# Gating the second batch's opening behind the first batch's scores, with an early Ln and an identity burst on TensorE, in an MoE–attention–MoE kernel

## The chip, the cores and the metric

The kernel runs on one core of a Trainium2 chip. The metric is the device time of one execution in microseconds (us); lower is better. The figures for the kernel before are three runs, and one more execution that was profiled. Engines are TensorE (PE; its weight loads are PEld), VectorE (DVE), ScalarE (ACT), GpSimd (POOL) and SyncE (SP, here only a DMA queue).

## What is computed

x is 8 batches of 512 rows with 128 features, all in float32. Three residual steps follow each other:

```python
x = x + 0.5 * ffn(layernorm(x), gate_w, fc_w, proj_w)   # 8 experts, each row uses its best 2
x = x + attention(layernorm(x), Wq, Wkv, Wout, bout, rel_emb)
x = x + 0.5 * ffn(layernorm(x), gate_w, fc_w, proj_w)

q = (x @ Wq) ...            # 16 heads of 64
k, v = split(x @ Wkv)       # one k and one v of 64 columns, shared by all heads
sim = q k^T * scale + bias  # bias by relative position, causal mask
out = softmax(sim) v ; out @ Wout + bout
```

The change touches the passage from the first step to the second: the opening of the attention.

## The kernel before, in words

**The expert stages** (`ffn_sp`, `ffn_pool`, `ffn_act`, `ffn_dve`, `ffn_pe`, called with 0 and with 1) sort all rows by expert into 72 tiles of 128 rows, and run up-projection (L1363), Gelu (L834), down-projection (L1373) and a copy (L1120, signalled by `yo_done`) tile by tile. In the first of them each result tile goes to `y1_dram`.

**The attention** is cut into small tasks, named by kind, batch b and place. The kinds that matter here, with engine and line:

- `GA(b,q)` on POOL (L762): two indirect gathers per 128 rows of a batch, which fetch the rows' two expert results into `yg`; the buffer holds one batch, so `GA(b+1)` waits for `CB(b)`.
- `CB(b,z)` on DVE (L1213, L1218): adds the weighted results to `x_sb`, four instructions for each half of a batch.
- `LS(b)` (DVE, L913 to L935) takes the row statistics and signals `ln_var`; `LA(b)` (ACT, `ln_act`, L803 and L805) takes Ln and Exp of the variance; `LN(b)` (DVE, L942 to L946 and L1231) makes the normalised rows `xa`.
- `BO(b)` on POOL (L769): adds the output bias to `x_sb`.
- `xT(b)` (PE, L1404) transposes `xa`; `xTh` (ACT, L859) and `xTl` (DVE, L1235) split the result in a high and a low part.
- `K`, `V`, `Q(b,g,c)` (PE, L1296 to L1298, three matmuls for each product) and their copies `KH`, `VC`, `QH` (ACT, L862, L865, L869) and `KL`, `QL` (DVE, L1238, L1243).
- For each of 16 units n (four head groups g, in each four row tiles t): `S` (PE, L1431) makes scores of four heads, `TTR` (DVE, L1253) adds the bias and takes the maximum, `EXP` (ACT, L874), `R` (DVE, L1260) the reciprocal of the sums, `N` (POOL, L789) the normalisation, `T` (PE, L1440) the transposes, `TC` their copy (ACT L881 or DVE L1266), `AV` (PE, L1456), `O` (ACT, L887), `Y` (PE, L1463), `YA` (DVE, L1275).

**The order of the work** is written out by a planner when the kernel is built. `attention_tasks` lists each task with a cost and with what it needs. `attention_order` walks through time with these costs: whenever an engine is free it gives it, of the tasks whose needs are met, the one with the smallest due time from `wanted_at`. The due time of `CB(1)`, `LS(1)` and `LN(1)` lies far behind that of the scores of batch 0, but a task with met needs is started at once when its engine is free. The result, `ORDER`, is one fixed list for each engine. On the chip each engine follows its list strictly, and waits on semaphores for the data of the other engines; the needs listed in the planner shape the lists, and the semaphore waits in the code are those of the data. Scores take two of four PSUM banks called "front", which K, V, Q and xT also use.

PE's list begins right behind `ffn_pe(0)`; ACT's behind the last Gelu; POOL's behind a wait for the last write of `y1_dram`.

Of the kernel before, what the change touches and what calls it, by code (L numbers as in the profile page):

```python
# [9 lines left out]
P = 128  # L10
D = 128
BATCH, SEQ = 8, 512
TILES = BATCH * SEQ // P
# [3 lines left out]
ETILES = TILES * TOPK + E  # L17
PAIRS = TILES * TOPK
H, DH = 16, 64
HG, NG = 4, 4  # L20
QT = SEQ // P
# [25 lines left out]
ACT = mybir.ActivationFunctionType  # L47
# [24 lines left out]
def build(nc, x, Wq, Wkv, Wout, bout, rel_emb, gate_w, fc_w, proj_w, out):  # L72
    ctx = ExitStack()
    with ctx:
        def sb(name, shape, dt=F32):
            return ctx.enter_context(nc.sbuf_tensor(name, shape, dt))

        def sem(name):
            return ctx.enter_context(nc.semaphore(name))
# [11 lines left out]
        ident = sb("ident", [P, P])  # L91
# [16 lines left out]
        lnt = sb("lnt", [P, 6, TILES])  # L108
# [4 lines left out]
        eps_t = sb("eps_t", [P, 1])  # L113
# [62 lines left out]
        with att:  # L176
# [33 lines left out]
        bank = [ctx.enter_context(nc.psum_tensor(f"bank{i}", [P, 512], F32)) for i in range(8)]  # L210
# [10 lines left out]
        ln_var = sem("ln_var")  # L221
# [12 lines left out]
        xrT_ps, xrT_done, up_ps, gelu_done, y_ps, yo_done = (  # L234
            sem(n) for n in ("xrT_ps", "xrT_done", "up_ps", "gelu_done", "y_ps", "yo_done"))
# [62 lines left out]
        def attention_tasks():  # L298

            tasks = {}  # L300

            def task(name, cost, needs, takes=None, frees=None, banks=1):
                tasks[name] = (cost, needs, takes and (takes, banks), frees if frees is None or type(frees[0]) is tuple else (frees, 0))

            for b in range(BATCH):
                for q in range(QT):
                    task(("GA", b, q), {"pool": 2.6}, [("CB", b - 1, q // 2)])
                for z in range(2):
                    task(("CB", b, z), {"dve": 1.6}, [("GA", b, 2 * z), ("GA", b, 2 * z + 1)])
                task(("LS", b), {"dve": 2.6}, [("CB", b, 0), ("CB", b, 1), ("LN", b - 1)])  # L310
                task(("LA", b), {"act": 3.4}, [("LS", b)])
                task(("LN", b), {"dve": 2.0}, [("xT", b - 1), ("LA", b)])
                task(("BO", b), {"pool": 1.3}, [("LN", b)])
                task(("xT", b), {"pe": 0.45}, [("LN", b), ("Q", b - 2, NG - 1, 1), ("V", b - 2), ("K", b - 2)], "front")
                task(("xTh", b), {"act": 0.48}, [("xT", b), ("Q", b - 2, NG - 1, 1), ("V", b - 2), ("K", b - 2)])
                task(("xTl", b), {"dve": 0.6}, [("xTh", b)], None, ("xT", b))
                task(("K", b), {"pe": 0.7}, [("xTl", b)] + [("S", b - 2, NU - 1, c) for c in range(2)], "front")
                task(("KH", b), {"act": 0.48}, [("K", b)] + [("S", b - 2, NU - 1, c) for c in range(2)])
                task(("KL", b), {"dve": 0.6}, [("KH", b)], None, ("K", b))
                task(("V", b), {"pe": 1.1}, [("xTl", b), ("AV", b - 2, NU - 1)], "front")  # L320
                task(("VC", b), {"act": 0.3}, [("V", b), ("AV", b - 2, NU - 1)], None, ("V", b))
                for g in range(NG):
                    for c in range(2):
                        b2, g2 = (b, g - 2) if g >= 2 else (b - 1, g - 2 + NG)
                        task(("Q", b, g, c), {"pe": 0.7}, [("xTl", b), ("S", b2, g2 * QT + QT - 1, c)], "front")
                        task(("QH", b, g, c), {"act": 0.5}, [("Q", b, g, c), ("S", b2, g2 * QT + QT - 1, c)])
                        task(("QL", b, g, c), {"dve": 0.6}, [("QH", b, g, c)], None, ("Q", b, g, c))
                for n in range(NU):
                    g, t = divmod(n, QT)
                    for c in range(2):  # L330
                        task(("S", b, n, c), {"pe": (0.34, 0.34, 0.5, 0.66)[t]},
                             [("KL", b), ("QL", b, g, c), ("T", *earlier(b, n, 8), t)], "front", None, 2)
                    for h in range(HG):
                        task(("TTR", b, n, h), {"dve": (0.28, 0.41, 0.55, 0.68)[t]}, [("S", b, n, h // 2), ("EXP", *earlier(b, n, 2), h)],
                             None, (("S", b, n, h // 2), h % 2))
                        task(("EXP", b, n, h), {"act": (0.385, 0.49, 0.6, 0.71)[t]}, [("TTR", b, n, h), ("R", *earlier(b, n, 8))])
                    task(("R", b, n), {"dve": 0.12}, [("EXP", b, n, h) for h in range(HG)] + [("N", *earlier(b, n, 8))])
                    task(("N", b, n), {"pool": (1.25, 2.1, 2.95, 3.8)[t]}, [("R", b, n)])
                    for jj in range(t + 1):
                        task(("T", b, n, jj), {"pe": 0.44}, [("N", b, n)], "turned")  # L340
                        task(("TC", b, n, jj), {"act": 0.48, "dve": 0.6}, [("T", b, n, jj), ("AV", *ring_user(b, n, jj))],
                             None, ("T", b, n, jj))
                    task(("AV", b, n), {"pe": 0.43 * (t + 1) + 0.05}, [("TC", b, n, jj) for jj in range(t + 1)] +
                         ([("VC", b)] if n == 0 else []) + [("YA", *earlier(b, n, 2))])
                    task(("O", b, n), {"act": 0.36}, [("AV", b, n), ("Y", *earlier(b, n, 2))])
                    task(("Y", b, n), {"pe": 0.45}, [("O", b, n)])
                    task(("YA", b, n), {"dve": 0.25}, [("Y", b, n), ("BO", b)])
                for q in range(QT):
                    task(("ST", b * QT + q), {"dve": 0.25}, [("YA", b, NU - QT + q)])
            for i, group in enumerate(GROUPS):  # L350
                task(("V2", i), {"dve": 1.7}, [("ST", t) for t in group])
                task(("A2", i), {"act": 3.4}, [("V2", i)])
                task(("I2", i), {"dve": 1.0}, [("A2", i)] + [("SC", t - 2 * QT) for t in group])
                for t in group:
                    task(("X2", t), {"dve": 0.34}, [("I2", i)])
                    task(("SC", t), {"pool": 2.6}, [("B2", i, 1)])
                mine = [m for m, piece in enumerate(PIECES) if piece[0] in group]
                for m in mine:
                    task(("T2", m), {"pe": 0.5}, [("X2", t) for t in PIECES[m]] + [("L2", m - 1)], "front")
                    task(("C2", m), {"act": 0.48}, [("T2", m), ("L2", m - 1)], None, ("T2", m))  # L360
                    task(("L2", m), {"pe": 0.6}, [("C2", m)], "front")
                    task(("G2", m), {"dve": 0.2}, [("L2", m), ("H2", i - 1, 1)], None, ("L2", m))
                task(("H2", i, 0), {"dve": 1.2}, [("G2", m) for m in mine] + [("B2", i - 1, 1), ("W3", i - 1)])
                task(("H2", i, 1), {"dve": 1.6}, [("H2", i, 0)])
                task(("W2", i), {"act": 0.25}, [("H2", i, 1)])
                task(("W3", i), {"dve": 0.6}, [("W2", i)])
                task(("P2", i), {"pe": 0.3}, [("H2", i, 1)], "front")
                task(("B2", i, 0), {"dve": 1.5}, [("P2", i)], None, ("P2", i))
                task(("B2", i, 1), {"dve": 1.2}, [("B2", i, 0)])
            return {k: (cost, [x for x in needs if x in tasks], takes, frees) for k, (cost, needs, takes, frees) in tasks.items()}  # L370
# [426 lines left out]
        def _(act):  # L797
            a = nc.scalar
# [35 lines left out]
                        a.activation(hT[:, n % 2, :], bank[2 + n % 2][:], ACT.Gelu).then_inc(gelu_done, 1)  # L834

            def attention_act():
                for k in ORDER["act"]:
                    kind, b = k[0], k[1]
                    if kind == "LA":
# [26 lines left out]
                    elif kind == "QH":  # L866
                        _, _, g, c = k
                        act.wait_ge(misc_ps, MISC_PS["Q", b, g, c])
                        a.activation(qst[:, g % 2, 0, c, :], BANK_OF["Q", b, g, c][:], ACT.Copy, scale=DH ** -0.5).then_inc(misc_hi, 1)  # L869
                    elif kind == "EXP":  # L870
                        _, _, n, h = k
# [4 lines left out]
                    elif kind == "TC":  # L876
                        _, _, n, jj = k
# [4 lines left out]
                    elif kind == "O":  # L882
                        _, _, n = k
# [405 lines left out]
        def _(pe):  # L1289
            t_ = nc.tensor  # L1290
# [85 lines left out]
                        ins.then_inc(y_ps, 1)  # L1376

            def attention_pe():
                for k in ORDER["pe"]:
                    kind, b = k[0], k[1]  # L1380
                    if k in BANK_OF:
# [33 lines left out]
                    elif kind == "Q":  # L1415
                        _, _, g, c = k
# [3 lines left out]
                    elif kind == "S":  # L1420
                        _, _, n, c = k
# [6 lines left out]
                        for i, (zq, zk) in enumerate(((0, 0), (0, 1), (1, 0))):  # L1428
                            for o in range(2):
                                rows = slice(o * DH, (o + 1) * DH)  # L1430
                                ins = t_.matmul(out[o][:, 0:w], qst[rows, g % 2, zq, c, t * P:(t + 1) * P], kst[rows, b % 2, zk, 0:w],  # L1431
                                                start=(i == 0), stop=(i == 2))
                                if i == 2:
                                    ins.then_inc(s_ps, 1)
                    elif kind == "T":
                        _, _, n, jj = k
# [5 lines left out]
                    elif kind == "AV":  # L1442
                        _, _, n = k
# [9 lines left out]
                        for jj in range(n % QT + 1):  # L1453
                            for o in range(2):
                                heads = pT[:, (b * NB + blk(n, jj)) % RING, :].rearrange("p (c o q) -> p o c q", c=2, o=2)[:, o, :, :]
                                ins = t_.matmul(BACK_BANK[n % 2][o * DH:(o + 1) * DH, 0:2 * P], vst[:, b % 2, jj, :], heads,  # L1456
                                                start=(jj == 0), stop=(jj == n % QT))
                        ins.then_inc(av_ps, 1)
                    elif kind == "Y":
                        _, _, n = k  # L1460
                        pe.wait_ge(ot_done, OT_DONE["O", b, n])
                        for c in range(2):
                            ins = t_.matmul(BACK_BANK[n % 2][:, 2 * P:2 * P + D], ot[:, n % 2, c * P:(c + 1) * P], wo_sb[:, n // QT, c, :],  # L1463
                                            start=(c == 0), stop=(c == 1))
# [26 lines left out]
```

## Time and profile before

| | |
|---|---|
| median of three runs | 1161.58 us (1161.24 to 1164.48) |
| the profiled execution | 1159.88 us |
| its span in the trace | 1157.9 us |
| PE, DVE, ACT, POOL busy, share of the span | 82%, 65%, 52%, 54% |
| mean granted TensorE clock | 0.938 of full speed |
| first expert stage | ends at 243.5 us of the span |
| attention | about 245 to 975 us |
| second expert stage and combination | to 1157.9 us |

The span is what the profiler saw of the profiled execution, 2.0 us less than that execution's time. "idle before" in a row names what ended an engine's wait. Shares over the whole span mix stages with different limits; the opening of the attention takes some 35 us of the 1157.9.

### The profile page before, as it was taken

The page shows a single profiled execution, that of the slowest core. Times are in us where ns is not written, and L with a number is a line of the kernel's source. Part 1 is how long each engine was busy: PE and PEld are TensorE (multiplying, and loading weights), DVE is VectorE, ACT ScalarE, POOL GpSimd, SP SyncE. Part 2 cuts the span into 40 slices and gives each one's busy share as a digit, 9 for nine tenths or more (in the row PEclk, how much of TensorE's full clock was granted, in tenths as well). Part 3 has the DMA queues.
Part 4 walks back from the last instruction along what each step waited for, and adds up shares of the span by engine and source line. Part 5 has one row for each costly group of instructions (what it writes and reads, how often), then busy time and mean ns, then how long its engine had stood idle before and what let it go on. Part 6 is the DMA issues. An engine that isn't in the chain of part 4 may idle for free.

```text
span 1157.9 us, 25233 instructions
## 1 busy us (share of the span) xinstructions
PE 949.3 (82%) x7670; PEld 771.9 (67%) x7670; DVE 755.4 (65%) x2652; ACT 603.8 (52%) x1627; POOL 623.1 (54%) x578
## 2 busy tenths in 40 slices
PE   1514999935989999899999899999898881999970
PEld 1514999934666767667777667776676661999970
DVE  4682222226898788978788897778878865333327
ACT  1201333314867777767788768777577661333320
POOL 2153445437677873448745559654486552455543
PEclk9996999976999999999999999999999995999995
DMA  7898888831457775200000000000000001777646
GB/s 206 127 99 256 209 211 208 200 82 44 72 90 124 126 123 105 39 5 32 4 2 2 1 13 27 2 2 1 2 29 11 1 20 51 209 204 210 202 135 198
DMA packets 105951, 106.57 MB, mean 92 GB/s; under 512 B 10034, under 2 KB 77748, under 8 KB 105824
## 3 DMA queue, kind: packets, MB, share of 16 engines
q1 hardware_dynamic: 96720, 86.41, 31.6%
q0 software_dynamic: 9104, 18.57, 7.2%
q8 instruction: 67, 1.10, 0.4%
q14 instruction: 60, 0.49, 0.2%
HBM read 65.22 MB, written 40.24 MB: 91 GB/s over the span
## 4 chain that ended last, share of the span: by engine, by line
PE 58%; DVE 19%; issue 7%; DMA 7%; SPq 3%; POOL 2%; ACT 2%; another core or an unknown queue 1%; DVEq 1%; POOLq 0%; ACTq 0%
PE bank L1431 11%; PE bank L1363 9%; PE bank L1440 9%; PE bank L1373 9%; PE bank L1456 8%; PE bank L1463 4%; DMA yg<-y_dram,pos_row 2%; DVE prob L1253 2%; DVE pT L1266 1%; PE bank L1296 1%; DMA xr<-slot_dram 1%; PE bank L1298 1%; PE bank L1297 1%; DVE x_sb L1131 1%; POOL yg L762 1%
## 5 line engine op out<-in xcount | busy, mean ns | idle before, releaser
L789 POOL TENSOR_TENSOR prob<-prob,rsum 128x256 f32<-128x256 f32 (+3 forms) x256 | 315.1, 1257 | 214.0 <-DVE rsum L1260 213.4
L874 ACT ACTIVATE prob<-prob,negmax 128x384 f32<-128x384 f32 (+3 forms) x512 | 282.4, 553 | 102.8 <-DVE negmax L1253 101.8
L1253 DVE CUSTOM_DVE_ANT_0 prob<-bank,bias_tab 128x384 f32<-128x384 f32 (+3 forms) x512 | 232.5, 484 | 55.5 <-PE bank L1431 52.6
L834 ACT ACTIVATE hT<-bank 128x512 f32<-128x512 f32 x144 | 86.0, 597 | 255.4 <-PE bank L1363 255.4
L1431 PE MATMUL bank<-kst,qst 64*128 64x256 f32 (+2 forms) x1536 | 182.4, 356 | 29.0 <-DVE negmax L1253 13.3
L1440 PE MATMUL bank<-ident,prob 128*128 128x128 f32 x1280 | 185.6, 279 | 3.4 <-ACT pT L881 3.2
L1431 PEld LDWEIGHTS bank<-kst,qst 64*128 64x128 f32 x1536 | 118.8, 191 | 86.4 <-issue 50.5
L1440 PEld LDWEIGHTS bank<-ident,prob 128*128 128x128 f32 x1280 | 145.2, 142 | 35.5 <-issue 17.3
L1120 DVE COPY yo<-bank 128x128 f32<-128x128 f32 x144 | 42.0, 291 | 194.0 <-PE bank L1373 181.5
L1456 PE MATMUL bank<-pT,vst 128*64 128x256 f32 x1280 | 165.5, 393 | 1.0 <-DVE pT L1266 0.9
L1363 PE MATMUL bank<-xrT,w1t 128*128 128x128 f32 x1152 | 155.0, 278 | 2.9 <-DMA w1t<-L_ffn_fc_w 2.3
L1373 PE MATMUL bank<-w_sb,hT 128*128 x1152 | 152.1, 275 | 0.0
L1363 PEld LDWEIGHTS bank<-xrT,w1t 128*128 128x128 f32 x1152 | 142.7, 195 | 3.4 <-issue 2.6
L1373 PEld LDWEIGHTS bank<-w_sb,hT 128*128 128x128 f32 x1152 | 140.2, 192 | 0.1
L1266 DVE COPY pT<-bank 128x512 f32<-128x512 f32 x167 | 113.5, 684 | 10.6 <-PE bank L1440 9.0
L1456 PEld LDWEIGHTS bank<-pT,vst 128*64 128x64 f32 x1280 | 82.8, 138 | 52.9 <-issue 18.0
L723 POOL DMA_INDIRECT xr<-xn_dram,gidx x72 | 68.3, 948 | 86.5 <-PE bank L1355 67.7
L730 POOL DMA_INDIRECT y_dram<-yo,sidx x72 | 70.8, 983 | 77.8 <-DVE sidx L1112 71.5
L881 ACT ACTIVATE pT<-bank 128x512 f32<-128x512 f32 x153 | 88.9, 589 | 29.5 <-PE bank L1440 28.8
L874 ACT ACTIVATION_READ_ACCUMULATOR prob<-prob,negmax 128x1 f32 x512 | 96.8, 189 | 0.0
L1463 PE MATMUL bank<-wo_sb,ot 128*128 128x128 f32 x512 | 85.3, 295 | 1.4 <-ACT ot L887 1.4
L779 POOL DMA_INDIRECT slot_dram<-slot,idx x64 | 63.4, 991 | 39.0 <-DVE idx L1207 22.6
(213 smaller groups left out, 1157.3 us busy)
## 6 DMA issues: line engine op xcount, KB each, us to landing
w1t<-L_ffn_fc_w SPq DMA_DIRECT2D x144, 256.0 KB
slot_dram<-fill SPq DMA_DIRECT2D x15, 975.0 KB
bias_dram<-hg SPq DMA_DIRECT2D x1, 5120.0 KB, 54.7
xr<-slot_dram SPq DMA_DIRECT2D x72, 65.0 KB
y_dram<-yo SPq DMA_DIRECT2D x72, 64.0 KB
bias_tab<-bias_dram SPq DMA_DIRECT2D x1, 4096.0 KB, 13.1
in_tile<-y_dram SPq DMA_DIRECT2D x8, 512.0 KB, 4.7
slot_dram<-fill SPq DMA_DIRECT2D x2, 1040.0 KB
```

The source lines that it names most:

```text
L789: g.tensor_tensor(out=pv, in0=pv, in1=rsum[:, n % 8, hs].unsqueeze(2).to_broadcast([P, 2, (n % QT + 1) * P]), op=ALU.mult).then_inc(norm_d ...
L834: a.activation(hT[:, n % 2, :], bank[2 + n % 2][:], ACT.Gelu).then_inc(gelu_done, 1)
L874: a.activation(prob[n % 8][:, h, :], prob[n % 8][:, h, :], ACT.Exp, scale=-1.0, bias=negmax[:, i % 8:i % 8 + 1], accum_out=lsum[:, n % 8, ...
L881: a.activation(pT[:, (b * NB + blk(n, jj)) % RING, :], BANK_OF["T", b, n, jj][:], ACT.Copy).then_inc(pt_act, 1)
L1253: v.tensor_tensor_reduce(out=prob[n % 8][:, h, :], in0=BANK_OF["S", b, n, h // 2][h % 2][:, 0:w], in1=bias_tab[:, HG * (n // QT) + h, SEQ ...
L1266: v.tensor_copy(pT[:, (b * NB + blk(n, jj)) % RING, :], BANK_OF["T", b, n, jj][:]).then_inc(pt_dve, 1)
L1363: ins = t_.matmul(bank[2 + n % 2][:, c * P:(c + 1) * P], w1t[:, n % 4, c * P:(c + 1) * P], xrT[:, n % 2, :], start=True, stop=True)
L1373: ins = t_.matmul(bank[6 + n % 2][:, 0:D], hT[:, n % 2, c * P:(c + 1) * P], w2_sb[:, ds(e, 1), c, :].rearrange("p a d -> p (a d)"), start= ...
L1431: ins = t_.matmul(out[o][:, 0:w], qst[rows, g % 2, zq, c, t * P:(t + 1) * P], kst[rows, b % 2, zk, 0:w], start=(i == 0), stop=(i == 2))
L1440: ins = t_.transpose(out[:, h * P:(h + 1) * P], prob[n % 8][:, h, jj * P:(jj + 1) * P], ident[:])
L1456: ins = t_.matmul(BACK_BANK[n % 2][o * DH:(o + 1) * DH, 0:2 * P], vst[:, b % 2, jj, :], heads, start=(jj == 0), stop=(jj == n % QT))
L1463: ins = t_.matmul(BACK_BANK[n % 2][:, 2 * P:2 * P + D], ot[:, n % 2, c * P:(c + 1) * P], wo_sb[:, n // QT, c, :], start=(c == 0), stop=(c ...
```

## The change

Four edits. In the planner, `CB(1,z)` also needs `QL(0,0,1)` and `KL(0)`; `BO(0)` also needs `KL(0)`; `xT(1)` also needs `N(0,4)`, the normalisation of the first unit of the second head group. ACT's list is preceded by one Ln of the 128x1 tile `eps_t` into a cell of `lnt`. PE's list is preceded by 12 matmuls of the identity with itself into bank 7, behind a wait for the last `yo` copy and for `LS(0)` (`ln_var` 2). The `GA` tasks of batch 2 need `CB(1)` as before, and so come later too.

```diff
@@ attention_tasks
                 for z in range(2):
-                    task(("CB", b, z), {"dve": 1.6}, [("GA", b, 2 * z), ("GA", b, 2 * z + 1)])
+                    opened = [("QL", 0, 0, 1), ("KL", 0)] if b == 1 else []
+                    task(("CB", b, z), {"dve": 1.6}, [("GA", b, 2 * z), ("GA", b, 2 * z + 1)] + opened)
...
-                task(("BO", b), {"pool": 1.3}, [("LN", b)])
-                task(("xT", b), {"pe": 0.45}, [("LN", b), ("Q", b - 2, NG - 1, 1), ("V", b - 2), ("K", b - 2)], "front")
+                task(("BO", b), {"pool": 1.3}, [("LN", b)] + ([("KL", 0)] if b == 0 else []))
+                task(("xT", b), {"pe": 0.45}, [("LN", b), ("Q", b - 2, NG - 1, 1), ("V", b - 2), ("K", b - 2)] +
+                     ([("N", 0, QT)] if b == 1 else []), "front")
@@ attention_act
+                a.activation(lnt[:, 3, TILES - 1:TILES], eps_t[:], ACT.Ln, bias=eps_t[:, 0:1])
                 for k in ORDER["act"]:
@@ attention_pe
+                pe.wait_ge(yo_done, ETILES)
+                pe.wait_ge(ln_var, 2)
+                for _ in range(12):
+                    t_.matmul(bank[7][:, 0:P], ident[:], ident[:], start=True, stop=True)
                 for k in ORDER["pe"]:
```

## Rows read from the trace of the kernel before

**Rows 1.** Page, part 1: busy time, share and instructions of the engines.
```profile
PE 949.3 (82%) x7670; PEld 771.9 (67%) x7670; DVE 755.4 (65%) x2652; ACT 603.8 (52%) x1627; POOL 623.1 (54%) x578
```
**Rows 2.** Busy time by stretch: length, PE, PEld, DVE, ACT, POOL, clock, DMA.
```profile
243.50:265.00 21.50, 0.11 (x1) 0.14 (x2) 7.39 (x32) 1.78 (x3) 14.63 (x16) 0.59 0.18 48
278.80:345.00 66.20, 58.03 (x407) 41.13 (x408) 58.70 (x200) 45.86 (x140) 45.12 (x40) 0.87 0.42 75
345.00:880.00 535.00, 511.03 (x4097) 375.11 (x4096) 443.27 (x1535) 398.00 (x1171) 333.47 (x287) 0.98 0.19 35
```
**Rows 3.** Chain that ended last, 230 to 300 us: start, length, what.
```profile
264.55 2.60 DMA yg<-y_dram,pos_row
...
267.53 2.31 DVE x_sb L1218 x2
...
275.32 1.28 ACT L803
```
**Rows 4.** Timeline of ACT, 241 to 283 us: start, length, instruction, idle before.
```profile
241.89 1.28 ACT L803 ACT_TABLE_LOAD   x1
259.99 0.30 ACT L803 ACTIVATE lnt<-lnt,eps_t 128x4 f32<-128x4 f32 x1 [16.82 <-DVE lnt L935]
...
261.60 0.20 ACT L805 ACTIVATE lnt<-lnt 128x4 f32<-128x4 f32 x1
...
274.70 0.60 ACT L862 ACTIVATE kst<-bank 128x512 fp32r<-128x512 f32 x1 [0.65 <-PE bank L1298]
...
278.34 0.37 ACT L865 ACTIVATE vst<-bank 128x256 f32<-128x256 f32 x1
```
**Rows 5.** Timeline of DVE, 241 to 283 us.
```profile
262.31 0.61 DVE L1218 SCALAR_TENSOR_TENSOR x_sb<-yg,gw,x_sb 128x128 f32<-128x128 f32 x2
262.83 0.15 DVE L942 TENSOR_TENSOR lnt<-lnt 128x4 f32<-128x4 f32 x1
...
282.01 0.69 DVE L1235 TENSOR_TENSOR xTl<-bank,xTh 128x512 fp32r<-128x512 f32 x1
```
**Rows 6.** Timeline of PE, 241 to 283 us.
```profile
264.89 1.09 PE L1404 MATMUL bank<-ident,xa 128*128 128x128 f32 x4 [21.73 <-DVE xa L1231]
270.49 0.80 PE L1296 MATMUL bank<-xTh,wqs 128*128 128x512 f32 x1 [4.52 <-DVE xTl L1235]
...
275.76 0.47 PE L1296 MATMUL bank<-xTh,wqs 128*128 128x512 f32 x1
...
277.00 0.40 PE L1298 MATMUL bank<-xTh,wqs 128*128 128x512 f32 x1
278.80 0.63 PE L1431 MATMUL bank<-kst,qst 64*128 64x256 f32 x6 [1.41 <-issue]
280.64 0.66 PE L1404 MATMUL bank<-ident,xa 128*128 128x128 f32 x4 [1.21 <-DVE negmax L1253]
```
**Rows 7.** Page, part 5: the up-projection's matmuls.
```profile
L1363 PE MATMUL bank<-xrT,w1t 128*128 128x128 f32 x1152 | 155.0, 278 | 2.9 <-DMA w1t<-L_ffn_fc_w 2.3
```
**Rows 8.** Timeline of PE where the second expert stage begins.
```profile
981.68 1.92 PE L1363 MATMUL bank<-xrT,w1t 128*128 128x128 f32 x8
983.46 0.48 PE L1355 MATMUL bank<-ident,xr 128*128 128x128 f32 x1
...
985.98 1.06 PE L1363 MATMUL bank<-xrT,w1t 128*128 128x128 f32 x8
```
**Rows 9.** PE by stretch of 1 us: length, busy, granted clock, DMA.
```profile
274.00:275.00 1.00, 1.00 (x8) 0.75 0.12 33
984.00:985.00 1.00, 1.00 (x9) 0.76 0.81 200
```
**Rows 10.** Timelines of POOL and DVE: the bias addition, and two steps of LS(2).
```profile
268.09 1.27 POOL L769 TENSOR_TENSOR x_sb<-x_sb,bout_sb 128x512 f32<-128x512 f32 x1
...
299.92 1.20 DVE L926 TENSOR_TENSOR lnt<-stats 128x4 f32<-128x4 f32 x1
...
301.12 1.86 DVE L928 TENSOR_TENSOR lnt<-stats 128x4 f32<-128x4 f32 x1
```

## The prediction

> **What bounds the kernel now.** I read the engines' shares first. PE leads with 82% and no other engine passes 65% [rows 1], but that mean hides the stage at issue, so I went on to the busy time by stretch [rows 2]. From 345 to 880 us PE is busy 511 of 535 us: there PE bounds, and a head start that reaches that stretch should be kept. From the last expert copy to 265 us PE does nothing, while the first batch is fetched and normalised. From the first score (278.80) to 345 both PE (58.0 of 66.2 us) and DVE (58.7) are nearly full, and the granted clock averages only 0.87, so nearly 9 us of that stretch's full-clock work is missing.
>
> The chain of waits tells what holds the first scores back [rows 3]: a gather of batch 1 (264.55, 2.60 us), DVE's combination of batch 1 (267.53, 2.31 us), and later a table load for batch 1's Ln on ACT (275.32). None of the three belongs to batch 0. The timelines of ACT, DVE and PE [rows 4 to 6] show the same: each engine follows a fixed list, and batch 1 stands in it ahead of batch 0.
>
> **The change part by part.**
>
> *CB(1) behind KL(0).* The first Exp ends at 261.80 [rows 4], but DVE begins LN(0) at 262.83 behind CB(1,0) [rows 5]. Without it LN(0) starts at about 261.82, and the transposes, at 264.89 before [rows 6], could start at 263.88: 1.0 us. After xTh DVE then stood in CB(1,1) until 269.84. Without that, from transposes to the first Q takes what batch 1 needs from its own transposes to the end of xTl: 280.64 to 282.70, 2.06 us [rows 5, 6], and 0.04 us to start. Before it was 270.49 − 264.89 = 5.60 us. That is 3.5 us more.
>
> *Late LA(1).* It goes with CB(1). Before, ACT ended KH at 275.30, then ran Ln, Exp and two table loads of batch 1, and copied V only at 278.34 [rows 3, 4]. The scores start right behind that copy, at 278.80, because it frees a bank. K's low part needs 0.60 us on ACT for KH and 0.69 us on DVE for KL (xTl's price, same size) [rows 4, 5], with hops 1.34 us after K ends. So S could follow K by 1.4 us; before it was 278.80 − 274.68 = 4.1.
>
> *The early Ln.* The table load of the first Ln stands at 241.89, and the Ln itself waits until 259.99 with the table in place [rows 4]. The load was ahead of the wait already. The added Ln takes the load over and runs some 0.3 us in 16.8 us of idle time: 0 us either way, and as much as nothing if that cover went. The later Ln and Exp loads remain. The Trainium skill ("ScalarE: Activation LUTs", What ACT_TABLE_LOAD costs) puts a switch of tables at about 2.66 us; and it says under What happens when an exp ACTIVATE runs that the compiler places the load right before the activation. Read so, the early Ln would take 2.66 us out of batch 0's path and the sum below would be 1153.3 instead of 1156.0; the row at 241.89 speaks against it and is what I follow.
>
> *The identity burst.* A float32 matmul shows as two records: 1152 records [rows 7] for 72 tiles, 2 stages and 4 matmuls each. So 12 matmuls are 24 records. Eight cost 983.46 − 981.68 = 1.78 us at the low clock, and about 0.9 us at the high one (1.06 us with the last one's tail) [rows 8]. The burst starts with LS(0)'s end, at 260.0. All at the low level (1.2 GHz) it lasts 5.3 us. But the clock rose to the high level (2.4 GHz) about 2.8 us after such matmuls began at 981.68, and 4.0 us after the Q products began at 270.49 [rows 6, 8, 9]. With 4.0 us, 18 records run low and 6 high: 4.7 us, to 264.7. The transposes wanted 263.88, so the burst costs 0.8 us (0.3 to 1.4). In return Q, Q, K run high: three matmuls at 512 columns cost (277.00 − 275.76)/5 = 0.25 us each, so nine take 2.25 us [rows 6], where they took 4.2 us (270.49 to 274.68): 1.9 us won.
>
> *The first score*: 264.7 + 2.06 + 0.04 + 2.25 + 1.4 = 270.4 or 270.5. Before 278.80: **8.3 us earlier** (6.4 us if the clock has fallen again by then).
>
> *What is then behind it.* The moved work does not vanish. CB(1), eight instructions of 0.31 us by its undisturbed row (two in 0.61) [rows 5], is 2.5 us. LS(1) is about 1.9 us (258.05 to 259.96, by LA(0)'s start) [rows 4]. Both lay before 278.8 and come behind the first score: 4.4 us of DVE. They now also meet POOL. Beside BO(0) two L1218 took 2.3 us instead of 0.6 [rows 3, 5, 10], and BO(0) is released by the same KL(0) as CB(1): up to 1.8 us again. Two steps of LS(2) took 1.20 and 1.86 us [rows 10] where such a step takes 0.15 (L942) [rows 5]: 2.7 us, which I put on LS(1) and as bound on LN(1). Up to 7.2 us, down to 0 if POOL is idle just then; I take half, 3.6. Sum on DVE: 8.0 us. The Trainium skill ("GPSIMD Engine Reference", Specifications) says that the two engines share their way to SBUF and contend when a DVE instruction has two SBUF inputs; these three kinds have, the scores' L1253 reads PSUM. The rows at 267.53 and 301.12 agree.
>
> Against that DVE was idle 66.2 − 58.7 = 7.5 us of this stretch [rows 2]; I let half of it, 3.7, be filled. DVE alone would keep 8.3 + 3.7 − 8.0 = 4.0 us. PE alone would keep all 8.3: its work is only shifted (xT(1), K(1), V(1) were all behind 278.8), and from 281 on it ran at the low clock, part of which may be recovered. POOL's eight gathers of GA(2), about 1.25 us apart, move behind the scores as well; POOL is idle 21 of 66 us, and N has the earlier due time, so 0 us. SP's fills wait for output tiles and only shift. xT(1) behind N(0,4) asks for nothing near its use: batch 1's scores come some 80 us later.
>
> **Sum.** Between 4.0 and 8.3 I take 5.6, nearer DVE, since it is the fuller engine up to 345 us. Profiled execution 1159.9 − 5.6 = 1154.3; the median lies 1.7 higher, so 1156.0. About 0.3%, 3.5 us, is what a measurement here can tell from no change.
>
> **The rivals.**
>
> 1. *Forecast* (0.46): 8 us earlier scores, some 4 to 8 kept; 1153.5 to 1158.0.
> 2. *All kept and the clock too* (0.13). If the high level also holds behind the first score, part of the missing 9 us comes back: 8.3 + 3 = 11, 1150. For: no low-clock K(1) and V(1) in the first scores. Against: the first scores leave PE half idle until transposes come, and with such gaps the clock fell at 281.
> 3. *Given back on DVE, or a burst without effect* (0.24). If the clock doesn't rise in the burst or falls before Q, the burst ends at 265.3 and Q, Q, K take 4.2: 2.5 us of the gain go, 1158.5. If the stretched steps are at their bound, about the same. The planner also re-orders everything later, which may add or take some 3 us.
> 4. *Slower* (0.17): DVE as the wall. LS(1) and LN(1) sit in DVE's list amid TTR and wait on POOL's port for the full 7.2 us, none of the idle time is filled, and the clock is low at the scores: 6.4 − 4.4 − 7.2 = −5.2, so 1166.8. It decides from the point at which moved and stretched work outgrow the 6.4 to 8.3 us. For: DVE is already the fullest engine there. Against: its idle time lies right behind the first scores.
>
> That the early Ln does nothing is part of all of them.
>
> **How the numbers follow.** Faster takes case 1 nearly whole and case 2: 0.58. Same is case 3, with the edge of case 1: 0.25. Slower is case 4: 0.17. The likeliest case gives 1156.0. The range reaches from case 2 (1149.5) to just short of case 4's price (1165.0).
>
> **What would show it.** Ln's table load at about 241.9 as before. 24 identity records from 260.0, the clock rising at 263 to 264. Transposes at 264.7, first Q near 266.8 and no L1213 ahead of it. First score at 270 to 271. CB(1) beside BO(0), with L1218 stretched. DVE nearly full from 271 to 340, and every later landmark (first AV, last AV of the attention) some 5 us earlier. The prediction is wrong if the first score is early but the last AV isn't, or if the burst is still running when xa is ready by more than 1.5 us.

## The result, and the profile after

| | before | after |
|---|---|---|
| median of three runs | 1161.58 us | 1150.08 us (1149.36 to 1152.96) |
| profiled execution | 1159.88 us | 1152.96 us |
| its span | 1157.9 us | 1151.1 us |
| mean granted clock | 0.938 | 0.948 |

The ratio is 0.9893, with a 95% interval of 0.9871 to 0.9916: the change makes the kernel 11.5 us faster, where 5.6 were forecast. The profiled execution of after was the slowest of its three, so the two traces differ by only 6.8 us of span.

The opening, engine by engine, from the profile of each execution. ACT and POOL of the changed kernel first (start, length, instruction, idle before it); line numbers have moved by two to seven against those of before.

```profile
242.94 1.28 ACT L839 ACT_TABLE_LOAD   x1
244.24 0.29 ACT L839 ACTIVATE lnt<-eps_t 128x1 f32<-128x1 f32 x1
260.93 0.30 ACT L805 ACTIVATE lnt<-lnt,eps_t 128x4 f32<-128x4 f32 x1 [16.39 <-DVE lnt L938]
...
266.98 0.60 ACT L862 ACTIVATE xTh<-bank 128x512 fp32r<-128x512 f32 x1 [4.24 <-PE bank L1411]
...
271.99 0.39 ACT L868 ACTIVATE vst<-bank 128x256 f32<-128x256 f32 x1 [0.66 <-PE bank L1301]
```
```profile
266.58 1.27 POOL L771 TENSOR_TENSOR x_sb<-x_sb,bout_sb 128x512 f32<-128x512 f32 x1
273.37 0.96 POOL L764 DMA_INDIRECT yg<-y_dram,pos_row  x1 [5.51 <-DVE x_sb L1221]
```

The table load stands where it stood before [rows 4], just behind the last Gelu; only its owner is new. V's copy (271.99) no longer waits behind batch 1's Ln and Exp. The bias addition BO(0) runs at 266.58, some five microseconds *ahead* of the KL(0) that it "needs" (271.36, below): a need in the planner shapes lists, and in POOL's list BO(0) stands right behind the gathers of batch 1.

DVE and PE of the changed kernel, the same columns:

```profile
262.84 0.16 DVE L945 TENSOR_TENSOR lnt<-lnt 128x4 f32<-128x4 f32 x1 [1.95 <-ACT lnt L807]
...
267.61 0.69 DVE L1238 TENSOR_TENSOR xTl<-bank,xTh 128x512 fp32r<-128x512 f32 x1 [2.85 <-ACT xTh L862]
...
271.36 0.69 DVE L1241 TENSOR_TENSOR kst<-bank,kst 128x512 fp32r<-128x512 f32 x1
271.97 0.60 DVE L1216 SCALAR_TENSOR_TENSOR x_sb<-yg,gw,x_sb 128x128 f32<-128x128 f32 x2
272.49 0.61 DVE L1221 SCALAR_TENSOR_TENSOR x_sb<-yg,gw,x_sb 128x128 f32<-128x128 f32 x2
...
284.75 1.86 DVE L929 TENSOR_TENSOR lnt<-stats 128x4 f32<-128x4 f32 x1
```
```profile
261.04 5.46 PE L1385 MATMUL bank<-ident 128*128 128x128 f32 x24 [16.82 <-DVE lnt L938]
266.29 0.65 PE L1411 MATMUL bank<-ident,xa 128*128 128x128 f32 x4
268.35 0.50 PE L1299 MATMUL bank<-xTh,wqs 128*128 128x512 f32 x1 [1.41 <-DVE xTl L1238]
...
272.66 0.62 PE L1438 MATMUL bank<-kst,qst 64*128 64x256 f32 x6
```

On DVE, ACT and PE no instruction of batch 1 is left between LS(0) and KL(0); POOL's gathers of batch 1 still run there. The first half of CB(1) follows KL(0) at once and stands ahead of the first score, the second half comes at 275.86, both at their undisturbed price. The burst ran wholly at the low clock; Q ran high (three records in 0.70 us). The first score stands at 272.66. This execution's first expert stage, untouched by the change, ended 1.06 us later (last `yo` copy at 244.26, before at 243.20), so I count from there: the first score came at 35.6 us before, and comes at 28.4 us.

To see where the time goes from there I take landmarks: the starts of the first, fourth, 16th, 32nd, 64th, 104th and last of the 128 output additions YA (L1275 of before), in us from the start of the last `yo` copy. They are read from the traces by their place in DVE's list, one traced execution for each kernel.

| | first score | tile 1 | tile 4 | tile 16 | tile 32 | tile 64 | tile 104 | tile 128 |
|---|---|---|---|---|---|---|---|---|
| before | 35.6 | 60.9 | 81.6 | 139.1 | 220.6 | 385.5 | 596.2 | 710.7 |
| after | 28.4 | 43.7 | 64.9 | 123.3 | 205.9 | 372.5 | 583.3 | 701.7 |
| lead | 7.2 | 17.2 | 16.7 | 15.8 | 14.7 | 13.0 | 12.9 | 9.0 |

The lead at the first score more than doubles until the fourth tile, and is then slowly paid back.

How much of such a lead is chance can be read from kernels of the experiments below whose four lists are those of before as far as tile 16 (e7, e11, and e4 but for its one early Ln). Their fourth tile came at 85.3 (e7), 82.9 (e11) and 85.3 us (e4), where the table has 81.6; their tile 32 at 222.7, 223.1 and 223.2, where it has 220.6. The clock differed: after the end of the expert stage it first rose at about 294 us of the span in e4 and e7, and at 274.5 in before. Four traces of the changed opening (after, e1, e8, e12) lie within 1.0 us at tile 4. So the trace of before is the quickest of its kind, and a lead over it is a low reading by up to 3.7 us at tile 4 and 2.6 at tile 32.

The same passages by the busy time of the engines (length, PE, PEld, DVE, ACT, POOL, clock, DMA share, GB/s): to the first score, to tile 4, to tile 16, to tile 32. Before:

```profile
243.20:278.80 35.60, 7.99 (x31) 6.17 (x32) 16.02 (x57) 7.61 (x13) 25.19 (x27) 0.62 0.18 48
278.80:324.80 46.00, 39.64 (x263) 28.25 (x265) 38.94 (x136) 31.74 (x95) 29.09 (x26) 0.85 0.30 56
324.80:382.30 57.50, 54.49 (x424) 39.12 (x425) 50.93 (x168) 41.75 (x122) 43.67 (x41) 0.94 0.73 122
382.30:463.80 81.50, 78.00 (x625) 57.06 (x623) 68.87 (x234) 60.86 (x186) 54.67 (x48) 0.98 0.66 114
```

After:

```profile
244.26:272.70 28.44, 10.25 (x54) 9.26 (x54) 9.70 (x35) 4.84 (x9) 16.40 (x17) 0.70 0.16 42
272.70:309.10 36.40, 31.14 (x249) 21.56 (x248) 34.68 (x127) 29.46 (x91) 29.34 (x26) 1.00 0.38 71
309.10:367.60 58.50, 56.43 (x449) 41.06 (x447) 55.93 (x187) 45.49 (x129) 44.14 (x42) 1.00 0.70 119
367.60:450.20 82.60, 78.73 (x625) 56.17 (x624) 70.42 (x243) 62.67 (x188) 63.02 (x56) 0.98 0.71 121
```

The second passage is where the forecast went wrong. It shrank from 46.0 to 36.4 us; PE is busy 8.5 us less in it and DVE 4.3 us less, and the clock is at its high level (2.4 GHz) throughout. DVE is now the fuller engine there, busy for 34.68 of 36.40 us. The third and fourth passages are each about 1 us longer.

What left the second passage is seen by the same kind of landmark. Before, K(1) and V(1) ran in it (V's copy at 44.7), and so did LS(2) and, at 78.2, the xa of LN(2). After, V(1) is copied at 111.0, CB(2) begins at 60.4 instead of 32.7 (it moved *into* the passage), and LN(2) comes at 96.1, behind tile 4. The gates name only batches 0 and 1; they pushed *everything* that runs ahead back by a step. They also re-ordered batch 0 itself: before, PE's list had the first transpose behind S(0,3,0) and the first AV behind Q(0,2,0); after, the first transpose stands behind S(0,2,1) and the first AV ahead of Q(0,2,0).

### The profile page after: what moved, and what is told of

It reads as the page before. It is cut to its first block, busy times and chain, and to the rows that moved or that the text cites. A ratio compares the mean times of both kernels' runs of the same rounds, so it can differ in the third digit from the quotient of the medians.

```text
span 1151.1 us, 25281 instructions
## 1 busy us (share of the span) xinstructions
PE 951.7 (83%) x7694; PEld 773.8 (67%) x7694; DVE 752.4 (65%) x2650; ACT 605.7 (53%) x1630; POOL 623.2 (54%) x578
## 4 chain that ended last, share of the span: by engine, by line
PE 61%; DVE 19%; issue 7%; DMA 4%; SPq 3%; ACT 2%; POOL 1%; another core or an unknown queue 1%; DVEq 0%; POOLq 0%; ACTq 0%
PE bank L1438 11%; PE bank L1447 10%; PE bank L1366 10%; PE bank L1463 9%; PE bank L1376 9%; PE bank L1470 4%; DVE prob L1256 2%; DVE x_sb L1216 2%; PE bank L1299 2%; DMA xr<-slot_dram 1%; PE bank L1301 1%; PE bank L1300 1%; DVE x_sb L1134 1%; DVE pT L1269 1%; PE bank L1358 1%
## 5 line engine op out<-in xcount | busy, mean ns | idle before, releaser
L1438 PE MATMUL bank<-kst,qst 64*128 64x256 f32 (+2 forms) x1536 | 179.1, 351 | 29.8 <-DVE negmax L1256 15.0
L1447 PE MATMUL bank<-ident,prob 128*128 128x128 f32 x1280 | 188.4, 282 | 2.1 <-ACT pT L884 1.9
L1447 PEld LDWEIGHTS bank<-ident,prob 128*128 128x128 f32 x1280 | 146.3, 143 | 34.1 <-issue 18.4
L1269 DVE COPY pT<-bank 128x512 f32<-128x512 f32 x165 | 111.6, 683 | 12.3 <-PE bank L1447 10.8
L732 POOL DMA_INDIRECT y_dram<-yo,sidx x72 | 70.8, 984 | 79.2 <-DVE sidx L1115 72.8
```

What stands on the lines that cost most here:

```text
L1269: v.tensor_copy(pT[:, (b * NB + blk(n, jj)) % RING, :], BANK_OF["T", b, n, jj][:]).then_inc(pt_dve, 1)
L1447: ins = t_.transpose(out[:, h * P:(h + 1) * P], prob[n % 8][:, h, jj * P:(jj + 1) * P], ident[:])
```

## The experiments

Ratios are against runs of the kernel before on the same chip; a ratio is not the quotient of the two medians (for e1 0.9849 against 0.9868), so differences in us that are given from medians are a second, rougher reading. A tile or score is timed from the last `yo` copy, as above.

**The parts of the change.**

`e1_again` is the changed kernel unaltered.

> The changed kernel once more, on the chip of the three others. Measured so far: 11.5 us under the kernel before (0.9893). Every theory expects 9 to 14 us under it again.

Measured: 1149.28 against 1164.66 us, ratio 0.9849 (0.979 to 0.9909). That is a little more than the 9 to 14 us expected. Its lead was 17.3 us at tile 4, 15.5 at tile 32 and 12.3 at tile 128.

`e2_gates_only`:

```diff
-                a.activation(lnt[:, 3, TILES - 1:TILES], eps_t[:], ACT.Ln, bias=eps_t[:, 0:1])
...
-                pe.wait_ge(yo_done, ETILES)
-                pe.wait_ge(ln_var, 2)
-                for _ in range(12):
-                    t_.matmul(bank[7][:, 0:P], ident[:], ident[:], start=True, stop=True)
```

> The three gates in the planner alone, no early Ln and no burst. Theory A (the gates carry the gain, because batch 1's K and V products and its Ln no longer stand among the first scores; the clock follows by itself): 8 to 12 us under the kernel before, first score near 271 us plus the shift of the stage, clock high from about 276. Theory B (the burst carries a good part by holding the clock high through the first scores): 2 to 6 us under it, with low-clock slices between 270 and 290.

Measured: 1150.13 us against 1164.66, ratio 0.9864 (0.9804 to 0.9924), more than the 8 to 12 us of theory A. The gates carry the gain. PE by stretches of 5 us (length, busy, clock, DMA share, GB/s):

```profile
270.00:275.00 5.00, 5.00 (x24) 0.70 0.00 0
275.00:280.00 5.00, 2.95 (x27) 0.98 0.17 41
280.00:285.00 5.00, 4.91 (x30) 0.68 0.16 39
285.00:290.00 5.00, 4.31 (x30) 1.00 0.02 3
```

Without the burst Q and K run low and the clock falls once more at about 280. The first score comes at 29.7 instead of 28.4 us, tile 4 at 66.4 instead of 64.9 (after) or 64.3 (e1); but at tile 32 it is 205.7 against 205.9 and 205.1. The burst's microsecond is used up by then. The medians differ by 0.85 us, which these intervals can't tell from nothing.

`e3_burst_only` puts the burst alone on the lists of before:

```diff
             def attention_pe():
+                pe.wait_ge(yo_done, ETILES)
+                pe.wait_ge(ln_var, 2)
+                for _ in range(12):
+                    t_.matmul(bank[7][:, 0:P], ident[:], ident[:], start=True, stop=True)
```

> The burst alone on the lists of the kernel before. Theory A: within 1.5 us of the kernel before, since CB(1) and LA(1) still stand in the way and the clock falls again at the gap of 4 us before the first Q. Theory B: 3 to 6 us under it, clock high through 281 to 295 where it was low.

Measured: 1163.8 us against 1164.66, ratio 0.9998 (0.9967 to 1.0029). The clock rose, and fell again before the first Q:

```profile
265.00:270.00 5.00, 1.33 (x10) 0.84 0.20 52
270.00:275.00 5.00, 4.07 (x10) 0.50 0.16 39
```

`e4_ln_only` adds the early Ln alone:

```diff
             def attention_act():
+                a.activation(lnt[:, 3, TILES - 1:TILES], eps_t[:], ACT.Ln, bias=eps_t[:, 0:1])
```

> The early Ln alone. The prediction's reading of the row at 241.89 says 0 us (within 1). The reading by which the load stood in batch 0's path says 1.3 to 2.7 us under the kernel before.

Measured: ratio 1.0003 (0.9969 to 1.0036), median 1167.48 us with a wide spread (1157.47 to 1173.09). The early Ln is worth nothing that shows.

Two of the three gates are settled by the lists that the planner writes. Without the gate on BO(0), or without the one on xT(1), or with the CB(1) gate alone, it writes the same lists for PE, DVE, ACT and POOL as with all three. **The one edit that does anything to the lists is the gate on CB(1).**

**What in that gate pays.** `e5_stats_gate` leaves CB(1) ahead and gates LS(1):

```diff
-                task(("LS", b), {"dve": 2.6}, [("CB", b, 0), ("CB", b, 1), ("LN", b - 1)])
+                task(("LS", b), {"dve": 2.6}, [("CB", b, 0), ("CB", b, 1), ("LN", b - 1)] + ([("QL", 0, 0, 1), ("KL", 0)] if b == 1 else []))
```

> The kernel before with one need added, on LS(1) in place of CB(1): batch 1's combination stays ahead of batch 0's products, its statistics, Ln, normalisation, transposes and K, V products come behind KL(0) and QL(0,0,1). Theory A (of the 17 us by which the first output tile comes earlier in the changed kernel, 7 are the earlier first score and 10 are batch 1's steps that stood between first score and first output): first score about 3 us earlier than before (V's copy no longer waits for Ln and Exp), first output tile 12 to 14 us earlier, total 8 to 11 us under the kernel before. Theory C (what counts is CB(1) ahead of LN(0) and xTl(0)): under 4 us.

Measured: 1159.52 us against 1164.63, ratio 0.9957 (0.9936 to 0.9977): half of what was expected. First score at 33.6 us (2.0 earlier), tile 1 at 57.3 (3.6 earlier, where 12 to 14 were expected), tile 4 at 73.7 (7.9 earlier), tile 32 at 215.8 (4.8 earlier). Here K(1), V(1) and LN(2) left the passage from first score to tile 4, but xT(1) and xTl(1) did not.

`e9_transposes_gate` is the other cut, the gate on xT(1) alone:

```diff
                 task(("xT", b), {"pe": 0.45}, [("LN", b), ("Q", b - 2, NG - 1, 1), ("V", b - 2), ("K", b - 2)] +
+                     ([("N", 0, QT)] if b == 1 else []), "front")
```

> The kernel before with the third gate alone: xT(1) needs N(0,4), CB(1), LS(1), LA(1) and LN(1) stay ahead. First score unmoved (35.6 us behind the last expert copy). Theory A (the first score's head start and the removal of xT(1), K(1), V(1) from behind the first score are two separate gains, about 7 and 8 to 10 us): fourth output tile 8 to 10 us earlier than before, total 4 to 9 us under the kernel before. Theory D (the second gain comes from batch 1's DVE and ACT steps, not from PE's): under 3 us.

Measured: 1159.64 us against 1165.03, ratio 0.9953 (0.9924 to 0.9982). The first score is unmoved (35.3), tile 4 comes 11.7 us earlier (8 to 10 were expected); the lead is 6.8 us at tile 32. The passage from first score to tile 4, as above:

```profile
280.02:314.70 34.68, 32.27 (x234) 22.82 (x236) 30.82 (x126) 28.87 (x88) 25.04 (x24) 0.90 0.30 49
```

So it shrinks from 46.0 to 34.7 us with nothing gained ahead of it. There are two separate gains: the head start, 7.2 us, and batch 1's xT, K and V out of the first scores, 6.8 us once their debt is paid. The sum of 14.0 lies near the 14.7 that the change shows at tile 32, though traces of one opening differ by up to 2.6 us there.

The second gain is not PE's alone. With xT(1) went xTl(1), KL(1) and LN(2) on DVE, and the copies on ACT: PE is busy 7.4 us less and DVE 8.1 us less. A part of DVE's share is steps with two inputs in SBUF that were stretched beside a POOL instruction. Counted against the shortest time of the same instruction, they lost 5.7 us in the passage of before, 1.2 in that of e9, 5.4 in that of after. Before, then after:

```profile
319.11 1.82 DVE L943 SCALAR_TENSOR_TENSOR lnt<-lnt 128x4 f32<-128x4 f32 x1
```
```profile
304.68 2.92 DVE L1216 SCALAR_TENSOR_TENSOR x_sb<-yg,gw,x_sb 128x128 f32<-128x128 f32 x2
```

The first is a step of LN(2); the same step of LN(0) took 0.16 us at 263.02. It ended at 320.93, together with the normalisation that POOL had begun at 317.16 (to 320.91). The second is two instructions of CB(2); two of CB(1) took 0.60 us at 271.97. What removing the stretched steps alone would give was not tried.

`e6_clock_held` asks how much of the second gain is the clock. On the lists of before PE multiplies the identity at four places:

```diff
                     kind, b = k[0], k[1]
+                    if k in (("S", 0, 0, 0), ("S", 0, 0, 1), ("xT", 1), ("K", 1)):
+                        for _ in range(5):
+                            t_.matmul(bank[7][:, 0:P], ident[:], ident[:], start=True, stop=True)
```

> The lists of the kernel before; PE multiplies the identity five times before each of S(0,0,0), S(0,0,1), xT(1) and K(1), so that the clock should not fall at 281. Theory clock (the low clock from 281 to 295 is most of the 10 us between first score and first output): first output tile 4 to 6 us earlier, total 3 to 6 us under the kernel before. Theory order (the place of batch 1's steps in the lists is what costs): at most 1.5 us either way.

Measured: 1160.48 us against 1164.63, ratio 0.9975 (0.9955 to 0.9995): 4.1 us by the medians. First score to tile 4, then the same passage in e7, whose opening is that of before:

```profile
281.10:324.90 43.80, 38.76 (x294) 28.28 (x293) 38.80 (x133) 31.23 (x95) 28.78 (x26) 0.96 0.34 59
```
```profile
281.40:330.23 48.83, 42.04 (x260) 29.95 (x260) 39.63 (x132) 31.46 (x95) 28.30 (x25) 0.78 0.30 51
```

The clock's share went from 0.85 (0.78 in e7) to 0.96, the passage from 46.0 (48.8) to 43.8 us: 2.2 to 5.0 us, with the identities' own time in it. The lead over before was 2.0 us at tile 4 and 5.0 at tile 32. The two theories split it: the first tile came 2.0 us earlier, less than the clock theory asked (4 to 6), the total moved as it asked (3 to 6). So the clock is worth a few microseconds of the opening, and not the 9.6 by which the passage shrank.

`e15_pe_blocked` does the reverse. Into the changed kernel it puts PE work of the size of batch 1's, where the kernel before had it:

```diff
+                    if k == ("S", 0, 1, 1):
+                        for _ in range(21):
+                            t_.matmul(bank[7][:, 0:P], ident[:], ident[:], start=True, stop=True)
```

> The changed kernel with 21 more identity matmuls (42 records, about 4.7 us at the high clock, the size of xT(1), K(1), V(1) as they ran before) ahead of S(0,1,1), where the kernel before had K(1) and V(1). Theory A (PE work there delays the first scores, and the delay is kept): fourth tile 3 to 5 us later than in the changed kernel, total 2 to 5 us slower than it. Theory E (DVE, ACT or POOL bound the first scores, PE has room): under 1.5 us.

Measured beside `e13_changed_5`, the changed kernel on the same chip: 1180.91 against 1175.44 us (ratios to the kernel before 0.9967, 0.9937 to 0.9997, and 0.9937, 0.9912 to 0.9961). The block took

```profile
283.27 6.57 PE L1390 MATMUL bank<-ident 128*128 128x128 f32 x42
```

and tile 4 came at 76.9 instead of 72.8 us, tile 128 at 729.3 instead of 725.2: 4.1 us both times. PE work that stands between the first scores is paid, here to some six tenths of its length, and stays paid: none of it is made up by tile 128. The six tenths are a net figure. On this chip the clock was low through the first scores in both kernels, and the block itself raised it: to the high level at 286.7 us, within the block, where e13 had it only at 290.0; the passage's clock was 0.90 against 0.85. At a clock that is high anyway, as in after, the share is not measured.

**What the rest of the lists does.** The planner's order behind the opening changes with every edit. To price such a change alone, `e7_order_noise_before` and `e8_order_noise_after` change one planner cost, from batch 2 on, in the two kernels:

```diff
-                    task(("YA", b, n), {"dve": 0.25}, [("Y", b, n), ("BO", b)])
+                    task(("YA", b, n), {"dve": 0.25 if b < 2 else 0.27}, [("Y", b, n), ("BO", b)])
```

> The kernel before with a planner cost for YA of 0.27 in place of 0.25 from batch 2 on: the opening is the same, later lists differ in places. Measures what a mere re-ordering of the later lists does. If the gain of the change is the opening's, this stays within 3 us of the kernel before, and the first output tile does not move; if re-ordering alone can give 10 us, it may show here.

> The same in the changed kernel: YA at 0.27 from batch 2 on. If the gain is the opening's, it stays within 3 us of the changed kernel, 9 to 14 us under the kernel before. If the later lists' luck carries it, it falls out of that.

Both expectations missed, as to the totals. The kernel before went from 1164.63 to 1179.79 us (1.0119, 1.009 to 1.0148), the changed one to 1159.55 (0.9953, 0.9936 to 0.9971), some 10 us over its own result. In both, most of it comes between tiles 72 and 80, where the kernel before went from 35.8 to 48.0 us. Changed kernel, then `e8`, in that passage:

```profile
666.70:702.40 35.70, 35.51 (x291) 26.56 (x291) 31.67 (x120) 29.49 (x87) 27.29 (x26) 1.00 0.09 29
```
```profile
664.70:712.20 47.50, 44.84 (x317) 33.55 (x317) 37.07 (x127) 31.12 (x93) 32.66 (x31) 0.86 0.07 23
```

The later lists hold more PE work in this passage (317 records for 291), PE has gaps, and the clock drops to 0.86. A second draw, with 0.30 for 0.27:

> YA at 0.30 in the planner from batch 2 on, in the kernel before. First re-ordering of this kind cost 15 us. Expected within 0 to 20 us above the kernel before; opening unmoved.

> YA at 0.30 from batch 2 on, in the changed kernel. If the opening's gain of some 15 us (lead at the 32nd output tile) is there whatever the later lists are, it is 5 to 25 us under its partner of the kernel before, and the lead at the 32nd output tile is 14 to 16 us.

Measured, against 1165.03: 1170.5 us (1.004, 1.0013 to 1.0067) and 1156.42 us (0.9912, 0.9877 to 0.9948). The three pairs:

| later lists | before's opening | changed opening | difference |
|---|---|---|---|
| as they are (e1) | 1164.7 | 1149.3 | 15.4 |
| YA 0.27 | 1179.8 | 1159.6 | 20.2 |
| YA 0.30 | 1170.5 | 1156.4 | 14.1 |

Within each pair the lead at tile 32 is 15.5, 17.1 and 16.8 us. The opening's gain at tile 32 does not depend on the lists behind it; the total can move by 5 to 15 us through them.

**A later gate.** `e10_gate_later`:

```diff
-                    opened = [("QL", 0, 0, 1), ("KL", 0)] if b == 1 else []
+                    opened = [("N", 0, 1)] if b == 1 else []
```

> The changed kernel with CB(1) behind the second unit's normalisation N(0,1) in place of KL(0) and QL(0,0,1). Theory A: first scores a little less disturbed, fourth output tile within 2 us of the changed kernel's, total within the spread that re-ordering gives (10 us at most slower), no clear gain over the changed kernel.

Measured: 1147.52 us against 1165.03, ratio 0.9842 (0.98 to 0.9883), which might beat the changed kernel. So the two were measured on one chip, with a gate on ("N", 0, 3) as `e16_gate_n3`:

> The changed kernel, for comparison with the later gates on one chip: 12 to 16 us under the kernel before.

> CB(1) behind N(0,1). Its one comparison put it at 0.9842, the changed kernel at 0.9849 and 0.9893 in two others. Expected 0 to 3 us under the changed kernel.

> CB(1) behind N(0,3), the last unit of the first head group. First three tiles as early as with N(0,1) or earlier; but batch 1's work and the gathers of batch 2 crowd later: total between 3 us under and 8 us over the changed kernel.

On that chip every kernel was 20 to 30 us slower, the kernel before too (1185.27 us). Changed kernel 1175.44 us, ratio 0.9937 (0.9912 to 0.9961), 9.8 us where 12 to 16 were expected; gate on N(0,1) 1176.07, 0.9932 (0.9907 to 0.9957); gate on N(0,3) 1179.3, 0.9949 (0.9924 to 0.9973). The first two can't be told apart, so the 0 to 3 us expected of the later gate are not shown, and no version here is shown to beat the changed kernel.

## Why the prediction was wrong

**Bounds and culprits: right.** The three waits named from the chain were those of batch 1, and the gates took them away ahead of the first score.

**CB(1) and LA(1) out of the way: right, slightly high.** The first score came 7.2 us earlier, not 8.3. LN(0) started right behind Exp (262.84), the gap from transposes to Q was 2.06 us as reckoned. Two things were missing. The burst ran low to its end, 5.25 us up to the transposes where I had 4.7, so that they started 22.0 us behind the last `yo` copy instead of 21.5. And PE's list has V(0) and Q(0,1,0) ahead of the first score: it started at 272.66, when PE came free of them, 2.1 us behind K(0)'s end (270.53) where I had 1.4.

**The early Ln at 0: right.** The load stood at 242.94 with it and at 241.89 without, and e4 gives 1.0003. The Trainium skill ("ScalarE: Activation LUTs", Step-by-step: what each stage is for) says that the compiler places the load right before the activation. In the program it stands there, but on the chip it ran ahead of the Ln's wait, so the reading by which it lay in batch 0's path is refuted. The same page (What ACT_TABLE_LOAD costs) puts a switch of tables at about 2.66 us. The timeline of ACT in before decides for less: K's copy ended at 275.30, the load ran from 275.32 for 1.28 us, and the Ln began at 276.62.

**The burst: right in direction, and small.** Forecast was a delay of 0.8 us for 1.9 us of faster products. Shown: 1.3 us at the first score, none at tile 32, nothing by itself (e2, e3). It stands on the chain that ended last, with 5.46 us. It also took longer to bring the clock up than the 4.0 us reckoned: begun at 261.04, it was low to its end.

**The step that failed** is the sentence "PE alone would keep all 8.3: its work is only shifted (xT(1), K(1), V(1) were all behind 278.8)", the upper bound of the sum. They were behind it, but they did not shift with the first score. They left the passage from first score to tile 4 altogether: V(1)'s copy went from 44.7 to 111.0 us while tile 4 went from 81.6 to 64.9. So the lead was 16.7 us at tile 4 and 14.7 at tile 32, where this bound allowed 8.3. Of the 9.6 us by which the passage shrank, 8.5 are busy time of PE, fewer products and faster ones, and 1.1 its idle time. PE work that stands in the first scores was paid (e15: 4.1 us at tile 4 and at the end for a block of 6.6). Later the third passage, which now holds xT(1), K(1) and V(1), is only 1.0 us longer. Taken out alone, with what hangs on them on DVE and ACT, the three are worth 11.7 us at tile 4 and 6.8 at tile 32 (e9). Why there is so little to fill PE with among the first scores is my reading and not shown: PE's list is strict, and few transposes are ready yet. In both kernels most of its waiting in the passage is for DVE's maximum (3.9 us before, 3.5 after).

**The DVE sum had the same fault,** and it was the bound that I leaned on. I charged CB(1) and LS(1) to the passage, 8.0 us with POOL's contention, and credited nothing for what they displaced. In the measured passage DVE is busy 34.7 us, not more than the 38.9 of before. A half of CB(1) and the start of CB(2) came in, but LN(2), KL(1) and xTl(1) fell out, and LS(1) took the place of LS(2). The contention was real, and with 5.4 us larger than the 3.6 that I took: one step of LS(1) took 1.86 us, two of LN(1) 0.77 and 0.96, two of CB(2) 2.92 together. But the passage before had lost 5.7 us in the same way, so it was no new cost. CB(1) met no bias addition at all (BO(0) at 266.58): I had taken the planner's need for a wait on the chip; it is none.

**The rivals.** The second, "all kept and the clock too", gave 1150, which is the time measured. Its mechanism is shown in part: the clock did stay high, and holding it high on the old lists gave 2.0 us at tile 4 and 5.0 at tile 32 (e6), against the 3 reckoned. Its other term, 8.3 us from the first score and nothing from the work that leaves the first scores, has the fault of the forecast; that the sum came out at 1150 is luck. The mechanism of the slower one (DVE as the wall) is half right: DVE became the fullest engine, busy for 34.68 of 36.40 us in the second passage, but with less work in it than before, so nothing got slower. The allowance of "some 3 us" for re-ordering was far too small: two small cost edits moved the total by 5 to 15 us.

What stays open: how the second gain divides between PE's work, DVE's work with its stretched steps, the clock and the new order of batch 0; why the clock rises and falls at other places in two executions of the same opening; and how much of the 11.5 or 15.4 us is luck of the later lists. The lead falls from 12.9 us at tile 104 to 9.0 at tile 128 in the profiled execution of after, when the same program in e1 kept 12.3: this goes with the clock, which was 0.92 and 0.91 from 910 to 930 us in after, and 1.00 in e1.

## What to carry to other kernels

In the fill of a pipeline, price an instruction that stands between the first inputs and the first outputs at a good part of its length (six tenths net in the one block tried here), and the same instruction in the steady state at what the slack there leaves: moving it can be worth the difference, even where the engine that holds it looks half idle. When an item in a run-ahead chain is held back, list what moves with it one step further back, before charging its cost to the passage. And where a greedy planner writes the lists, draw two or three trivial variants of its costs before believing any total under one per cent. Read landmarks of several executions, too: one trace of the kernel before was 3.7 us off its fellows at tile 4.

## What the runs showed of the hardware

The clock fell in gaps of PE's work, as in the rows before: in e3 the burst raised it and 4.6 us without PE work lost it again before the first Q, while in the changed kernel, with 1.4 us between transposes and Q, it stayed at 1.00 up to 367.6 us. By these two runs the gap behind a burst decides whether it is of use; gaps between the two lengths were not tried.

Not expected was how different one chip can be. On the last one the changed kernel took 1175 us for 1149, with the first expert stage ending at 244.28 us as elsewhere. Its trace has 14 waits on ACT and DVE, 1.0 to 6.3 us each and 33.8 us in all, which the profile puts down to "remote", that is to no instruction of the program; the trace of e1 has none. The first of them, in `e13_changed_5`, against 4.24 us behind PE in the fence of ACT above:

```profile
269.06 0.60 ACT L862 ACTIVATE xTh<-bank 128x512 fp32r<-128x512 f32 x1 [6.30 <-remote]
```

The transposes had ended at about 266.8, so some 2.2 us have no cause in the trace; the first Q slipped to 270.43, the clock fell, and the first score came at 34.1 us. The head start is thereby fragile: of 11.5 to 15.4 us elsewhere 9.8 were left there by the medians, and 7.5 by the ratio. What causes the stalls was not tried.
